# Attention on one core: a pair's score variance one place up in two engines' order, and three experts loaded ahead of the gathers

## What is computed

```python
x = x + tanh(g_xattn[0]) * softmax(norm(sim) * ln_gamma + ln_beta)   # sim from layernorm(x) and ctx_512
x = x + tanh(g_ffn[0])   * moe0(layernorm(x))    # 8 experts, top 2, inner width 688
x = x + tanh(g_xattn[1]) * (0.6 * sigmoid(si + sj + b) + 0.4 * layernorm(x))
x = x + tanh(g_ffn[1])   * moe1(layernorm(x))    # 15 experts, top 2, inner width 176, and a shared one
```

## Time and profile before

| | us |
|---|---|
| median of 3 runs | 366.01 |
| lowest and highest | 364.84, 366.41 |
| the profiled execution's own time | 367.4 |
| its span, first to last instruction | 365.3 |
| TensorE busy | 315.0 (86%) |
| VectorE busy | 204.2 (56%) |
| ScalarE busy | 152.6 (42%) |
| GpSimd busy | 108.2 (30%) |

### The profile page before, as it was taken

One profiled execution on the slowest core, in us unless ns is written; L12 is line 12 of the kernel. 1 busy time (PEld: TensorE's weight loads), 2 busy tenths in 40 slices (PEclk: granted clock), 3 DMA queues, 4 the chain that ended last, 5 costly groups with the idle time before them and its releaser, 6 DMA issues.

```text
span 365.3 us, 6901 instructions
## 1 busy us (share of the span) xinstructions
PE 315.0 (86%) x2128; PEld 178.4 (49%) x2128; DVE 204.2 (56%) x639; ACT 152.6 (42%) x339; POOL 108.2 (30%) x106
## 2 busy tenths in 40 slices
PE   8975459899999999999999999158868998989992
PEld 6644444555555555555565555047324444434341
DVE  1678865755544455555545542495956445354247
ACT  1555431134443433433344444267433444455541
POOL 0021132122343322222212211133255555653310
PEclk9995556999999999999999999655899999999997
DMA  7999919996836462545221112401231222231146
GB/s 233 348 306 320 306 45 287 281 288 194 238 55 227 112 193 38 182 101 134 31 36 16 16 18 27 97 35 59 72 87 59 79 82 77 84 74 51 53 142 217
DMA packets 21209, 48.38 MB, mean 132 GB/s; under 512 B 2664, under 2 KB 11752, under 8 KB 20152
## 3 DMA queue, kind: packets, MB, share of 16 engines
q1 hardware_dynamic: 14744, 35.78, 31.3%
q0 software_dynamic: 6048, 11.28, 14.2%
q10 hardware_dynamic: 384, 0.90, 0.8%
HBM read 37.98 MB, written 9.96 MB: 131 GB/s over the span
## 4 chain that ended last, share of the span: by engine, by line
PE 71%; DVE 13%; DMA 5%; issue 5%; ACT 3%; POOL 1%; DVEq 1%; ACTq 0%; SPq 0%; POOLq 0%
PE bank L1461 27%; PE bank L1435 22%; PE bank L1511 6%; PE bank L1424 6%; PE bank L1272 3%; PE bank L1332 2%; PE bank L1280 2%; DMA wgu<-results 1%; DVE st L764 1%; DVE z L954 1%; DMA sums<-y_sb,route_dst 1%; DVE z L842 1%; PE bank L1353 1%; DMA rows<-sums 1%; DMA x_in<-rows,route_tok 1%
## 5 line engine op out<-in xcount | busy, mean ns | idle before, releaser
L1461 PE MATMUL bank<-wgu,xT 128*64 x320 | 99.6, 465 | 1.5 <-DVE xT L1053 0.9
L1461 PE MATMUL bank<-rows,xT 128*64 128x344 f32 x320 | 99.6, 465 | 0.0
L1435 PE MATMUL bank<-wdn,hT 120*64 (+2 forms) x396 | 88.3, 383 | 7.8 <-ACT wgu L703 2.6
L1435 PEld LDWEIGHTS bank<-wdn,hT 120*64 120x64 f32 (+1 forms) x396 | 47.7, 136 | 47.7 <-issue 19.2
L1461 PEld LDWEIGHTS bank<-wgu,xT 128*64 128x64 f32 x320 | 43.1, 140 | 47.5 <-issue 8.4
L430 POOL DMA_INDIRECT sums<-y_sb,route_dst x20 | 31.6, 1580 | 115.6 <-ACT y_sb L631 91.6
L422 POOL DMA_INDIRECT x_in<-rows,route_tok x43 | 42.4, 985 | 41.6 <-DVE route_tok L960 17.8
L1033 DVE SCALAR_TENSOR_TENSOR hh<-th,bank 128x344 f32<-128x344 f32 x40 | 20.5, 513 | 57.5 <-ACT th L578 57.4
L1435 PE MATMUL bank<-rows,hT 120*64 120x256 f32 x228 | 52.3, 379 | 0.0
L578 ACT ACTIVATE th<-bank 128x344 f32<-128x344 f32 x40 | 18.3, 457 | 60.8 <-PE bank L1461 60.0
L1461 PEld LDWEIGHTS bank<-rows,xT 128*64 128x64 f32 x320 | 43.1, 140 | 0.0
(11 more groups left out here) (173 smaller groups left out, 442.0 us busy)
## 6 DMA issues: line engine op xcount, KB each, us to landing
wgu<-gu SPq DMA_DIRECT2D x8, 1376.0 KB, 19.1
wdn<-wd SPq DMA_DIRECT2D x8, 720.0 KB, 22.9
wgu<-gu SPq DMA_DIRECT2D x3, 1408.0 KB
wdn<-wd SPq DMA_DIRECT2D x5, 576.0 KB
rows<-rows SPq DMA_DIRECT2D x8, 256.0 KB, 3.9
wgu<-results SPq DMA_DIRECT2D x8, 256.0 KB, 5.1
wgu<-gu SPq DMA_DIRECT2D x1, 1056.0 KB
rows<-xt SPq DMA_DIRECT2D x4, 256.0 KB, 7.3
```

Source lines behind the costliest of these rows:

```text
L1435: last = mm(psum[7][part, 0:H], inner[0:m.wide, j * P:(j + 1) * P][:, part], wd(j), start=(j == 0), stop=(j == m.chunks - 1))
L1461: last = mm(psum[2 * c + g][part, 0:CH0], xT[:, r, k * P:(k + 1) * P][:, part], w, start=(k == 0), stop=(k == KH - 1))
```

## The change

`AT_ONCE` becomes 3, so SP issues three experts' loads ahead of the stores and five behind the gathers. On GpSimd the power for the scores of pairs 1 and 2 stands in front of that for the rows of pair 0, and so on. On VectorE `score_norm` is cut in two (`scaled_scores`, `less_most`), the statistics leave `attend` (`x1_stats`), each pair's `score_var` stands one place further up, the constants follow the first `score_var`, and the router's centring stands behind `score_var(2)`.

```diff
-AT_ONCE = 4
+AT_ONCE = 3
...
             rstd(0, s_var, s_rstd, fs)
+            rstd(1, s_var, s_rstd, fs)
+            rstd(2, s_var, s_rstd, fs)
+            rstd(0, mix[0].var, mix[0].rstd)
+            rstd(3, s_var, s_rstd, fs)
             for b in range(1, B):
-                rstd(b, s_var, s_rstd, fs)
-                rstd(b - 1, mix[0].var, mix[0].rstd)
-            rstd(B - 1, mix[0].var, mix[0].rstd)
+                rstd(b, mix[0].var, mix[0].rstd)
...
             score_var(0)
-            score_norm(0)
-            score_var(1)
-            score_norm(1)
             (wait for gates_done, three instructions for edge_c)
+            scaled_scores(0)
+            score_var(1)
+            less_most(0)
+            scaled_scores(1)
+            less_most(1)
+            attend(0)
+            x1_stats(0)
+            score_var(2)
             centre_router()
-            attend(0)
-            for b in range(2, B):
-                score_var(b)
-                score_norm(b)
-                attend(b - 1)
-                norm_terms(b - 2)
-            attend(B - 1)
-            norm_terms(B - 2)
+            scaled_scores(2)
+            less_most(2)
+            attend(1)
+            score_var(3)
+            x1_stats(1)
+            norm_terms(0)
+            scaled_scores(3)
+            less_most(3)
+            attend(2)
+            x1_stats(2)
+            norm_terms(1)
+            attend(3)
+            x1_stats(3)
+            norm_terms(2)
```

More of the change, by code:

```diff
@@ L835, in score_var, with scaled_scores @@
                                                in1=floor[:, two], op0=ALU.mult, op1=ALU.add).then_inc(s_var, 1)
-            def score_norm(b):
-                tiles = (2 * b, 2 * b + 1)
+            def scaled_scores(b):
                 dve.wait_ge(s_rstd, b + 1)
-                for i in tiles:
+                for i in (2 * b, 2 * b + 1):
                     nc.vector.scalar_tensor_tensor(
@@ L844, in score_norm, with less_most @@
                         in1=vec_sb[:, V_BETA:V_BETA + N], op0=ALU.mult, op1=ALU.add).then_inc(z_made, 1)
-                for i in tiles:
+            def less_most(b):
+                for i in (2 * b, 2 * b + 1):
                     dve.wait_ge(z_made, i + 1)
@@ L862, in attend, with x1_stats @@
                         op0=ALU.mult, op1=ALU.add).then_inc(x1_made, 1)
+            def x1_stats(b):
                 dve.wait_ge(x1_made, 2 * b + 2)
```

## The result

Seven runs of the changed kernel give a median of 369.27 us (367.68 to 375.06), seven of the kernel before 366.02 (364.84 to 366.58); the ratio is 1.007, with an interval of 1.004 to 1.0101. The profiled execution took 369.65 us, its span is 367.7. So the change makes the kernel slower, by 3.3 us in the medians and 2.6 by the ratio, although the attention it reorders is faster. Both can be read from the trace.

The account below looks back on a forecast made before the run. VectorE with GpSimd was taken to bound 17 to 37 us, TensorE from 55 us on; -3.1 (order) + 3.8 (stall) + 2.4 (clock) = +3.1 us on 366.01 gave 369.1 us, range 364.2 to 371.0 for 8 in 10.

Parts of the forecast that it names:

- Part 1: Attention on VectorE and GpSimd: the new order shortens the waits before the scaled scores and wins 3.1 us.
- Rival 3: Attention: ScalarE or TensorE's half clock holds VectorE back, 1 to 2 us of the 3.1 go; 370.5 us, chance 0.08.
- Part 2: Three experts ahead: the fifth load behind the gathers lands late and TensorE stalls 3.8 us before tile 4's transposes.
- The landing: Last weight load behind the gathers: lands at 99.4 us, where the last one before landed at 91.4.
- the clock of before: Times given as in the earlier kernel's trace; in the changed kernel everything there was to start 3.1 us earlier.
- Rival 1: Weight loads land in time, mark at about 95.6, TensorE loses nothing: 362.9 us, faster; chance 0.14.
- The 8.0 us: Weight loads behind the gathers: time one more expert adds to the last landing, with bounds 7.6 and 8.9.
- the bulk rule: Last weight load, by volume alone: bulk over at 88.0 plus 7.6 puts the mark at 95.6, no stall.
- Part 3: TensorE's clock falls to half in or just behind the gap, which costs 2.4 us in the work after it.
- Rival 2: TensorE's stall comes but its clock holds: net +0.7 us, 366.7 us; chance 0.18.
- comes back sooner: TensorE behind the gap: a clock that has fallen late recovers earlier, so 2.4 us and not 2.9.
- What it removes: SP's queue: 2.15 MB of loads gone from in front of the stores of sums and rows, worth nothing by itself.

Follow-up runs that it names:

- e1: Changed kernel with four experts ahead of the gathers (AT_ONCE = 4), so the new order alone: 362.97 us, ratio 0.9917 to the kernel before.
- e2: Kernel before, old order, with only AT_ONCE set to 3: 373.53 us, ratio 1.0204 to the kernel before.
- e3: Changed kernel, but tiles 5 to 10 wait for their own expert's mark, not for all eight: 362.88 us, ratio 0.9920 to the kernel before.
- e7: Changed kernel with 11 unused matmuls on TensorE ahead of tile 4's transposes, to fill the gap: 369.46 us, ratio 1.0123 to the kernel before.
- e13: The kernel of e1 (changed kernel, four experts ahead) again, beside e12 on one chip: 362.39 us, ratio 0.9933 to the kernel before.
- e12: The kernel of e8 (changed kernel, fourth expert's loads right behind the last store) again, beside e13: 361.42 us, ratio 0.9921 to the kernel before.
- e4: Changed kernel, but VectorE's wait for the next tile's weights stands behind the hidden product: 367.00 us over 12 runs, ratio 1.0031 to the kernel before.
- e11: The kernel of e7 (changed kernel with 11 matmuls in the gap) again, beside e10 on one chip: 368.23 us, ratio 1.0100 to the kernel before.
- e6: The changed kernel measured a second time, with no edit: 370.46 us, ratio 1.0125 to the kernel before.
- e10: The changed kernel measured a third time, with no edit, beside e11 on one chip: 370.81 us, ratio 1.0137 to the kernel before.
- e8: Changed kernel, fourth expert's loads issued right behind the last store, four left behind the gathers: 362.02 us, ratio 0.9908 to the kernel before.
- e9: Changed kernel with the edits of e8 and e3 together: 362.36 us, ratio 0.9921 to the kernel before.

## Why the prediction was right

- **Part 1, 3.1 us.** Measured 3.2 from the first variance to the scores of pair 3 and on to the gather. The waits that were to be left, 0.7, 0.1, 0.7 and 0, are 0.70, 0, 0.69 and 0. Rival 3 didn't occur.
- **Part 2, the stall, 3.8 us.** The step was right: `weights_of` asks for all eight from tile 5 on, and VectorE's queue puts tile 4's product behind that wait. The landing, 99.4 on the clock of before, is 96.8 after the gather's own shift of 2.63; measured 97.06. The gap is 4.58, 0.8 more, partly from this and mostly because TensorE was 0.6 us further ahead than I had it. That the mark and not the order is the cause is shown by e1 (mark early, no gap), e2 (old order, a gap of 7.72) and e3 (mark late, nobody waits, no gap). Rival 1 needed a mark before 92.5; the earliest in any profile with five loads behind the gathers is 94.8.
- **How the landing was worked out.** The 8.0 us came out right in sum, its parts didn't. On the bulk rule the bytes would have ended at 93.0 (95.6 less 2.63). They ended near 94.9 (DMA share 0.96 at 92 to 94, 0.45 at 94 to 96), since from 84 to 94 us the engines moved 247 GB/s and not the 284 of the earlier trace rows. The tail between bulk and mark was about 2.2 us and not 3.4. The two errors nearly cancel in this profile. That one slow engine makes the tail is not shown by any trace here.
- **Part 3, the clock, 2.4 us.** It fell inside the gap and cost 2.26; with the gap filled it stayed up and 2.4 were saved in the same work (e7). Rival 2 fell. But the rows behind this part carry less than I took from them. In the row of 228.8 to 231.3 TensorE was still busy for 1.03 us, so it had been dry for 1.5 us when the clock fell, not 2.5; in e2 the clock stayed at 1.00 for 5.0 us of the gap. A gap of 3.8 us could have ended before a fall. And no row stood behind "comes back sooner", the reason for 2.4 in place of 2.9; the price was 2.0 to 2.4 in four profiles.
- **Where it was wrong.** "What it removes" was costed at nothing. With the attention earlier the stores of `rows` do hold up the first gather when four experts are ahead of them, by 1.2 us (e1, e13 against e12). The term was mis-sized, 0 for 1.2 us; the prediction's sum stands, since it had three ahead and the whole 3.1 in it. VectorE was to stand "about 4 us"; it stood 8.43, and the prediction's own numbers give 7.5 (from 91.90, the end of the copy of xT, to 99.4): 4 us is what TensorE loses. And the range for the landing, 7.6 to 8.9 us behind the mark before, was too narrow: it says nothing of how far the mark moves between executions.
- **The total.** The median, 369.1 against 369.27, is closer than its terms. In the profiled execution, 370.5 forecast and 369.65 measured, the attention began 0.6 late, the gap was 0.8 longer, the tiles in between won 0.6, and the second layer gave back 1.2 us that I hadn't counted. The same kernel measured later, 370.46 and 370.81, lay 4.8 and 6.4 us over the kernel before beside it (by the ratios 4.6 and 5.0), where +3.1 was forecast. The sign and the three steps are shown; that the median fits to 0.2 us is luck.

## What to carry to other kernels

Before an engine's stage is shortened, ask who has been given time by it: here the stores of `rows` ran on the time that attention took, and with four experts ahead 1.2 us of the gain went to them. The loads behind the gathers did not: they start with the second gather, and they stall the kernel with the old order too (e2). A wait for everything where one part is needed, placed in front of work for somebody else in an in-order queue, turns a late transfer into a stall of the bound engine, and TensorE's clock adds its own price to the gap, here 2.0 to 2.4 us for gaps of 4.6 to 8.6. When a load is taken from the front of a queue, look for the next idle hole of the DMA engines before leaving it for last.

## What the runs showed of the hardware that I had not expected

The last of the ten weight transfers is issued between 56.4 and 56.9 us in the changed kernel and in its variants with five loads behind the gathers. Its landing moves by 6.5 us between their profiles: 94.8 (e4), 96.5 (e7 and e11), 96.9 (e3), 97.06, 99.52 (e6) and 101.31 us (e10). e10 and e11 ran on one chip. With four loads behind the gathers (the kernel before, e1, e8, e9, e12, e13) the last took 30.4 to 33.2 us, with five 37.9 to 44.6. SP's waits of the two ends, e4 and e10 (us in total, times, longest):

```profile
SPq L347 <- DMA wdn<-wd: 37.3, 5, 8.6
```

```profile
SPq L347 <- DMA wdn<-wd: 43.8, 5, 10.9
```

The bulk of the bytes ends near 95 us in both the changed kernel's profile (DMA share 0.45 at 94 to 96, 0.03 at 96 to 98) and e10's (0.56, 0.16 and 0.06 in the three stretches from 94 to 100 us), and the mark follows about 2 us behind it in the first and 6 in the second. A share of 0.06 is what one of the 16 engines gives, so by an estimate one to three engines were still at work in e10's tail; the profile doesn't say which, nor with what. What holds back the last part of a transfer stays open; no run was made on it. A kernel that waits for this mark can take over its movement: the changed kernel's three profiled executions, with marks at 97.06, 99.52 and 101.31, took 369.65, 373.34 and 372.63 us, and e10 spreads over 6.8 us, while e3, which doesn't wait, spreads over 1.8. That the mark makes the whole of such a spread isn't shown: three profiles are few, and the last two times stand in the other order.
